# Moving roundings, weight splits, loads and transposes in a routed expert kernel

## What is computed

```python
x = x + cross(layernorm(x), ctx, mask)      # operands rounded to fp8, fp32 sum
h = layernorm(x)
idx, w = router(h)                           # 4 of 32 experts for each row
Xp = h[slots_token].reshape(E, C, d)         # E = 32 experts, C = 160 rows each
Y = (silu(Xp @ W_gate) * (Xp @ W_up)) @ W_down
out = zeros.at[slots_token].add(Y * slots_w)
shared = silu(h @ sg.T) * (h @ su.T) @ sd.T
x = x + out + shared
```

## Time and profile before

| | kernel before |
|---|---|
| executions, us | 1991.67, 1992.34, 1993.89 |
| the profiled execution, us | 1995.68 |
| its span, us | 1993.8 |
| TensorE clock granted, mean | 0.989 |
| PE busy, us (share of the span) | 1835.2 (92%) |
| DVE busy | 1390.6 (70%) |
| ACT busy | 865.1 (43%) |
| POOL busy | 601.7 (30%) |
| PE's share of the chain that ended last | 89% |

### The profile page before, as it was taken

The page is one execution under the profiler, slowest core; times in us unless marked ns, Lnnn a source line. Parts: engine busy times, 40 slices in busy tenths (PEclk is TensorE's granted clock), DMA queues, the critical chain, the costliest instruction groups (busy, mean ns, idle before and its releaser), DMA issues.

```text
span 1993.8 us, 44056 instructions
## 1 busy us (share of the span) xinstructions
PE 1835.2 (92%) x17380; PEld 1401.9 (70%) x17396; DVE 1390.6 (70%) x2509; ACT 865.1 (43%) x1209; POOL 601.7 (30%) x611
## 2 busy tenths in 40 slices
PE   0039999999999999999999999989999999999997
PEld 0017578668667767866866776778888888888886
DVE  5888685575566557557545644578888888888884
ACT  8564221222212212122221211357777777777773
POOL 2100211220220221122022022335655655656652
PEclk9989999999999999999999999999999999999999
DMA  9935534343433443434243245399999999999993
GB/s 377 395 96 171 148 72 109 100 102 86 106 97 75 106 118 69 112 97 103 67 106 75 54 106 143 82 344 365 353 368 360 353 370 358 354 370 349 366 367 82
DMA packets 188301, 395.45 MB, mean 198 GB/s; under 512 B 116304, under 2 KB 120432, under 8 KB 163600
## 3 DMA queue, kind: packets, MB, share of 16 engines
q1 hardware_dynamic: 163184, 334.77, 48.7%
q0 software_dynamic: 23808, 58.81, 13.5%
q10 hardware_dynamic: 1184, 0.15, 0.0%
HBM read 314.79 MB, written 55.35 MB: 186 GB/s over the span
## 4 chain that ended last, share of the span: by engine, by line
PE 89%; DVE 2%; issue 1%; DMA 1%; POOL 0%; ACT 0%; SPq 0%; DVEq 0%; POOLq 0%; ACTq 0%
PE ps L1334 54%; PE ps L1345 16%; PE ps L1517 8%; PE ps L1372 5%; PE ps L1525 2%; PE ps L1479 1%; PE ps L1420 1%; DVE W L1013 0%; DMA BIG<-in_w_gate 0%; PE ps L1484 0%; PE ps L1426 0%; DMA BIG<-in_sh_down 0%; POOL out_rows L606 0%; DVE BIG L941 0%; DVE BIG L940 0%
## 5 line engine op out<-in xcount | busy, mean ns | idle before, releaser
L1334 PE MATMUL ps<-XT,W 128*128 128x256 f16 (+1 forms) x12288 | 1114.2, 253 | 7.8 <-DVE SG L1302 3.8
L1334 PEld LDWEIGHTS ps<-XT,W 128*128 128x128 f16 x12288 | 1027.5, 98 | 92.0 <-issue 15.8
L1277 DVE SCALAR_TENSOR_TENSOR W<-BIG,W 128x2048 f16<-128x2048 f32 x192 | 435.9, 2284 | 64.7 <-ACT W L837 64.7
L837 ACT ACTIVATE W<-BIG 128x2048 f16<-128x2048 f32 x192 | 361.4, 1900 | 9.2 <-DMA BIG<-in_w_gate 8.8
L1345 PE MATMUL ps<-W,HH 128*128 128x512 f16 x1536 | 334.3, 379 | 1.8 <-DVE W L1013 1.8
L779 ACT ACTIVATE SG<-ps 128x256 f32<-128x256 f32 x128 | 49.0, 383 | 616.3 <-PE ps L1334 616.3
L1345 PEld LDWEIGHTS ps<-W,HH 128*128 128x128 f16 x1536 | 150.3, 98 | 182.9 <-issue 2.3
L257 POOL TENSOR_TENSOR expo<-expo 128x1 f32<-128x1 f32 x159 | 82.7, 520 | 633.0 <-ACT FR L708 266.5
L1192 DVE SCALAR_TENSOR_TENSOR SG<-ps,SG 128x256 f32<-128x256 f32 x128 | 54.2, 424 | 239.0 <-ACT SG L779 239.0
L539 POOL TENSOR_TENSOR rs<-ve,expo 128x1 f32<-128x1 f32 x32 | 17.6, 549 | 566.0 <-DVE ve L1034 566.0
L596 POOL DMA_INDIRECT FR<-xn_rows,gix x64 | 166.4, 2601 | 30.0 <-issue 30.0
(11 more groups left out here) (178 smaller groups left out, 1629.7 us busy)
## 6 DMA issues: line engine op xcount, KB each, us to landing
BIG<-in_w_gate SPq DMA_DIRECT2D x64, 1024.0 KB, 9.1
BIG<-in_w_up SPq DMA_DIRECT2D x64, 1024.0 KB, 8.2
BIG<-in_w_down SPq DMA_DIRECT2D x64, 1024.0 KB, 8.3
X<-in_x SPq DMA_DIRECT2D x16, 1024.0 KB, 5.0
X<-in_mask POOLq DMA_DIRECT2D x16, 1024.0 KB, 8.2
xn_rows<-FR SPq DMA_DIRECT2D x32, 512.0 KB, 3.6
out_rows<-X SPq DMA_DIRECT2D x32, 512.0 KB, 3.5
W<-in_x SPq DMA_DIRECT2D x6, 2048.0 KB, 19.6
```

Source lines behind the costliest of these rows:

```text
L837: ac.activation(dst, stage, ACT.Copy, scale=W_SCALE).then_inc(x_hi, 1)
L1277: ve.scalar_tensor_tensor(out=lo[cut], in0=src, scalar=W_SCALE, in1=hi[cut], op0=ALU.mult, op1=ALU.subtract).then_inc(x_lo, 1)
L1334: ins = te.matmul(out_ps, a[:, k, cols], b[:, k, :], start=n == 0, stop=n == len(steps) - 1)
```

## The change

In group 0, `x_round` moves from steps 4 and 5 to 3 and 4, the pieces 7 and 8 get steps of their own (2 and 3; 7 was at 1, and 8 was with 9 at step 5), 13 and 14 go from behind `residual` to step 7, and piece 12 is loaded ahead of SP's wait for the roundings. At the seam, expert 1's weights 0 to 3 are loaded ahead of the two stores of group 15 and 4 and 5 behind them, the gather of expert 0 goes ahead of four of POOL's index operations, the transposes of expert 0 go between matmul 15 and 16 of the last down product (u = 3), and `et_lo(0)` goes ahead of the last `add_shared`.

```diff
--- before.py
+++ after.py
@@ -280,7 +280,7 @@
         SW_PIECES = [(m, k, 4, ih) for ih in range(2) for m in range(2) for k in (0, 4)]
         SW_PIECES += [(2, k, 2, nh) for nh in range(2) for k in (0, 2, 4, 6)]
 
-        FIRST_SPLITS = [(4, 5), (6, 7), (), (), (), (8, 9), (10,), (11, 12), (13, 14, 15)]
+        FIRST_SPLITS = [(4, 5), (6,), (7,), (8,), (9,), (10,), (11, 12), (13, 14), (15,)]
         sw_dram = [sh_gate, sh_up, sh_down]
 
         LOADS = [("x", 0), ("b", 0), ("x", 1), ("x", 2), ("b", 1), ("x", 3), ("c", 0), ("x", 4), ("c", 1), ("x", 5),
@@ -385,6 +385,10 @@
             ctx_load(9, 1)
             ctx_load(8, 0)
 
+            def ew_load(e, m):
+                src = rows((w_gate, w_up, w_down)[m // 2], (e * 2 + m % 2) * P, P)
+                sp.dma_start(ew_stage[m], src).then_inc(ld_ew[m], 16)
+
             def xn_stores(f):
                 for j in range(NT):
                     wait(sp, a_xn, 2 * f + j + 1)
@@ -410,9 +414,10 @@
                     x_load(g + 1, 1 - r)
                 if first:
                     sw_load(11)
+                    sw_load(12)
                     sp.wait_ge(d_q, 4)
                     xq_transposes(1)
-                    for n in range(12, 16):
+                    for n in range(13, 16):
                         sw_load(n)
                     xn_stores_and_transposes(1)
                 if front and not first:
@@ -429,6 +434,11 @@
                 if front and not first:
                     xn_stores_and_transposes(g + 1)
                 for j in range(NT):
+                    if not front:
+
+                        for m in (2 * j, 2 * j + 1):
+                            sp.wait_ge(x_lo, m + 1)
+                            ew_load(1, m)
                     wait(sp, d_out, 4 * g + 2 * j + 2)
                     sp.dma_start(rows(out, g * G + j * P, P), xbuf[r][:, j, :]).then_inc(st_out[r], 16)
 
@@ -441,10 +451,6 @@
             for g in range(10, GROUPS - 1):
                 group(g, g % 2, ctx=max(12 - g, 0))
 
-            def ew_load(e, m):
-                src = rows((w_gate, w_up, w_down)[m // 2], (e * 2 + m % 2) * P, P)
-                sp.dma_start(ew_stage[m], src).then_inc(ld_ew[m], 16)
-
 
             sp.wait_ge(pe_xa, 4 * GROUPS)
             for m in range(6):
@@ -460,7 +466,10 @@
                 for c in range(TQ):
                     sp.dma_start(tab[c * TC:(c + 1) * TC, :, 1, :], slots[P:C]).then_inc(ld_tab, 16)
             group(GROUPS - 1, 1, front=False, ctx=0)
-            with sp.Fori(1, E) as e:
+            for m in (4, 5):
+                sp.wait_ge(x_lo, m + 1)
+                ew_load(1, m)
+            with sp.Fori(2, E) as e:
                 for m in range(6):
 
                     wait(sp, x_lo, e * 6 + (m - 5))
@@ -574,15 +583,9 @@
             ch.link(gp.tensor_scalar(tok[:, :], tab[:, :, 1, 0], float(T - 1), None, ALU.min))
             ch.do(gp.tensor_scalar(main(gidx[:, :]), tab[:, :, 0, 0], float(T - 1), None, ALU.min))
             ch.do(gp.tensor_scalar(tail(gidx[:, :]), tok[:, :], float(TQ), quarter[:, 0:1], ALU.mult, ALU.add))
-            ch.do(gp.tensor_copy(main(sidx[:, :]), tab[:, :, 0, 0]))
-            ch.do(gp.tensor_scalar(tail(sidx[:, :]), tab[:, :, 1, 0], float(TQ), quarter[:, 0:1], ALU.mult, ALU.add))
-            wts_cols = wts[:, :].rearrange("p (e u) -> p e u", u=3)
-            ch.do(gp.tensor_scalar(wts_cols[:, :, 0:2], tab[:, :, 0, 1].unsqueeze(2).to_broadcast([P, E, 2]), DOWN_PROJ, None,
-                                   ALU.mult))
-            ch.do(gp.tensor_scalar(wts_cols[:, :, 2], tab[:, :, 1, 1], DOWN_PROJ, None, ALU.mult))
             ch.sync()
             ch.close()
-            SLOT_STEPS = ch.before
+            GATHER_STEPS, SLOT_STEPS = ch.before, ch.before + 4
 
             def cols(e):
                 return bass.ds(e * 2, 2)
@@ -613,7 +616,15 @@
                 pool.wait_ge(st_xn[j], 16 * GROUPS)
             pool.wait_ge(d_lo, 2 * (GROUPS - 1))
             pool.wait_ge(t_xn, 64 * (GROUPS - 1))
-            gather(0, 0, SLOT_STEPS + 1, 2 * GROUPS)
+            gather(0, 0, GATHER_STEPS + 1, 2 * GROUPS)
+            ch.before += 1
+            ch.do(gp.tensor_copy(main(sidx[:, :]), tab[:, :, 0, 0]))
+            ch.do(gp.tensor_scalar(tail(sidx[:, :]), tab[:, :, 1, 0], float(TQ), quarter[:, 0:1], ALU.mult, ALU.add))
+            wts_cols = wts[:, :].rearrange("p (e u) -> p e u", u=3)
+            ch.do(gp.tensor_scalar(wts_cols[:, :, 0:2], tab[:, :, 0, 1].unsqueeze(2).to_broadcast([P, E, 2]), DOWN_PROJ, None,
+                                   ALU.mult))
+            ch.do(gp.tensor_scalar(wts_cols[:, :, 2], tab[:, :, 1, 1], DOWN_PROJ, None, ALU.mult))
+            ch.sync()
             gather(1, 1, SLOT_STEPS + 2, 2 * GROUPS + 1)
 
             for b in range(2):
@@ -1203,8 +1214,8 @@
                         route_picks()
                     if ic == (5 if front else 3):
                         route_weights()
-                    if front and ic - first in (3, 4):
-                        x_round(g + 1, ic - first - 3, M_main)
+                    if front and ic in (3, 4):
+                        x_round(g + 1, ic - 3, M_main)
                     if ctx and ic == 6 and not first:
 
                         ctx_round(g, 2 * g + 9, 1, 2 * g + 10)
@@ -1248,6 +1259,7 @@
                     ctx_round(0, 9, 1, 10)
                 if weights:
                     weights(3)
+                    et_lo(0)
                 add_shared(g, r, 3)
                 if first:
                     dve.wait_ge(d_cq, 10)
@@ -1287,7 +1299,6 @@
                 last = g == GROUPS - 1
                 group(g, g % 2, front=not last, ctx=max(12 - g, 0),
                       weights=(lambda n: ew_lo(0, 0, n)) if last else None)
-            et_lo(0)
             ew_lo(0, 0, 4)
             ew_lo(0, 0, 5)
 
@@ -1334,7 +1345,7 @@
                     ins = te.matmul(out_ps, a[:, k, cols], b[:, k, :], start=n == 0, stop=n == len(steps) - 1)
                 return ins
 
-            def down(out_ps, acts, weights, chunks, toks, cols, last_chunk=None):
+            def down(out_ps, acts, weights, chunks, toks, cols, last_chunk=None, between=None):
 
 
                 (hhi, hlo), (whi, wlo) = acts, weights
@@ -1342,6 +1353,8 @@
                 for n, (a, b, k) in enumerate(steps):
                     if last_chunk and n == 3 * (chunks - 1):
                         pe.wait_ge(*last_chunk)
+                    if between and n == 3 * (chunks // 2 + 1):
+                        between()
                     ins = te.matmul(out_ps, a[:, k, toks], b[:, k, cols], start=n == 0, stop=n == len(steps) - 1)
                 return ins
 
@@ -1399,6 +1412,24 @@
                         ins = te.transpose(PS[6 + h][:, k * P:(k + 1) * P], xn[j][:, (4 * h + k) * P:(4 * h + k + 1) * P],
                                            identf[:, :])
                     ins.then_inc(pe_xt, 1)
+
+            def et_transpose(e, b):
+
+                pe.wait_ge(ld_xg[b], (e - b) * 16 + 32)
+                for s in range(2):
+                    for k in range(4):
+                        ins = te.transpose(PS[2 + s][:, k * P:(k + 1) * P], xg[b][:, (4 * s + k) * P:(4 * s + k + 1) * P],
+                                           identf[:, :])
+                    ins.then_inc(x_xt, 1)
+                quarters = et_tail.rearrange("p (c q t) -> p q c t", c=TQ, q=2)
+                for q in range(2):
+                    ins = te.transpose(quarters[:, q], xgt[b][:, q * P:(q + 1) * P], identf[:, :])
+                ins.then_inc(x_xt, 1)
+
+            def first_rows():
+                pe.wait_ge(a_lg, GROUPS)
+                pe.wait_ge(d_route, GROUPS)
+                et_transpose(0, 0)
 
             def group(g, r, front=True):
                 if isinstance(g, int) and g == 0:
@@ -1450,7 +1481,8 @@
                         pe.wait_ge(sw_lo, 12 + 4 * u)
                     down(PS[4 + u % 2][:, :], hT, SW[2], KS, slice(j * P, (j + 1) * P),
                          slice(h * HALF, (h + 1) * HALF),
-                         last_chunk=(d_hl, 8 * g + 8) if u == 0 else None).then_inc(pe_dn, 1)
+                         last_chunk=(d_hl, 8 * g + 8) if u == 0 else None,
+                         between=first_rows if u == 3 and not front else None).then_inc(pe_dn, 1)
 
             pe.wait_ge(consts_ready, 2)
             for n, ready in ((0, x_root), (1, amax_ready)):
@@ -1470,24 +1502,6 @@
                 group(pair * 2 + 1, 1)
             for g in range(10, GROUPS):
                 group(g, g % 2, front=g < GROUPS - 1)
-
-            def et_transpose(e, b):
-
-                pe.wait_ge(ld_xg[b], (e - b) * 16 + 32)
-                for s in range(2):
-                    for k in range(4):
-                        ins = te.transpose(PS[2 + s][:, k * P:(k + 1) * P], xg[b][:, (4 * s + k) * P:(4 * s + k + 1) * P],
-                                           identf[:, :])
```

(10 more changed lines are left out.)

## The result

The changed kernel is faster, but by less than forecast. Thirteen timed executions beside thirteen of the kernel before gave medians of 1987.50 us and 1992.32 us, ratio 0.9979 with a 95% interval of 0.9972 to 0.9987. That is 4.8 us where 9.4 were forecast. The median lies above the span given with the forecast itself, 1981 to 1985, and inside the whole range of 1978.5 to 1988.0. Three later sets of executions of the same code gave 3.3, 3.3 and 2.9 us.

The account below looks back on a forecast made before the run. PE, busy 92% of the span, was taken as the bound, so only its standing or half clock could be won. Group 0's 2.2 plus the seam's 7.2 gave 9.4 us: median 1992.34 to 1982.9, range 1978.5 to 1988.0.

Parts of the forecast that it names:

- Group 0, the walk: Group 0: queues walked with measured durations; gain taken as 2.2 us, range -1 to 5.
- The stand at step 4: Group 0: PE newly stands 2.5 us near 175; costs nothing while DVE's queue is later, bound 0 to 1.
- the stand inside `cross`: Group 0: PE stands 4.3 us between the halves of cross, waiting for add_cross, and the clock falls.
- 8.6 us can be won: Seam: stretch from 1298.7 to 1329.5 takes 30.8 us against 22.2 undisturbed.
- the gain of 7.2: Seam: expert 1 starts at 1321.8 + 0.5 instead of 1329.5; range 1.5 to 7.7 us.
- The gather: Seam: gathered rows land at 1297.2, so PE stands 0.5 us ahead of expert 0's transposes, range 0 to 6.2.
- The mechanism I gave most room: Seam: DVE's ew_lo cast holds the first gather to 1291.9, so the second starts only 1.5 us earlier.
- The rule of the port: Seam: GpSimd cannot write descriptors while VectorE holds the shared port; first gather goes out about 1291.4, walk has 1291.9.
- The rule of the clock: PE: array falls to 1.2 GHz after an idle stretch; by it the 4.3 us stand must lose the clock.
- The clock holds: Rival, group 0: the clock holds or stands are split so it does; part gains 5, 1980.1 us; chance 0.12.
- The gather is late: Rival, seam: PE stands 3 us or more inside the down product; 1985.6 to 1991.6 us; chance 0.14.
- The second store: Rival, seam: store behind load 3 holds ACT and expert 0; 4 to 6 us slower, 1997; chance 0.04.

Follow-up runs that it names:

- the version that beats both: Changed kernel with pieces 7 and 14 moved back, loads 2 and 3 behind the second store, ACT's store wait moved to rows_out; 1978.28 against 1991.71 us.
- the loads held: Changed kernel with SP holding expert 1's loads 2 and 3 until expert 0's gathered rows have landed; 1990.24 against 1992.96 us.

## Why the prediction was wrong, point by point

**Group 0, the walk.** Right in its course. The stand at step 4 came (0.91, 3.69, 2.82, 2.86 us for 2.5 forecast), the transposes were no longer waited for, `add_cross` started at 206.02 (forecast 206.2), the stand inside `cross` was 4.75 us (4.3), group 1 started at 232.7 (233.9). The gain over four traces each is 2.3 us, forecast 2.2; over all traces with the old and the new group 0 (six and eight) it is 1.9, and the kernel with these edits alone gained 1.8 by its median (0 to 3.6). That it comes so near is in part luck: the walk's old cost (85.7) and its new one (83.7) both lie about 1 us above the means, 84.7 and 82.4, and that falls out of the difference. The walk said that the stand at step 4 costs nothing; in three of four traces it lost the clock for 3 to 7 us, and the second half of `cross` then started 0.4 to 1.2 us later than where the clock held. That is within the bound of 0 to 1 but for one.

**Group 0, what was not seen.** I took DVE's queue as given. Two entries of `FIRST_SPLITS` that the change had moved were costing some 4 us against what their old places allow (group 0: 78.4 and 78.6 us against a mean of 82.4; 75.3 in the version that beats both). The part's sum was right, and more than it forecast was left lying.

**The seam, the term that failed.** "8.6 us can be won", and from it the gain of 7.2. The walk of the seam after was nearly right: expert 1 started 46.4, 45.4, 45.2 and 45.4 us after group 15's down products began, where the walk has 44.4. What failed was the other side of the subtraction. The 51.6 us before rests on a stand of 3.84 us and the half clock behind it. In the other traces with that code the seam is 46.5 to 48.2: the first weights were there 5.7 to 7.5 us after their issue, where the prediction's trace had 9.1, and with stands of 0.4 to 2.2 us the clock was kept. This accounts for 3.9 us (51.6 against the 47.7 of the other three traces of the kernel), and the seam after, 45.6 us on average where the walk has 44.4, for another 1.2, most of it the late gather. What is left of the 7.2 is 2.1, and the kernel with the seam's edits alone gained 2.4.

There was a warning: the profiled execution took 1995.68 us, above each timed one, and it stayed above all thirteen of the comparison (highest 1993.89). I noted the 3.34 us and took the whole gain off the median all the same. A surplus of 3.3 us must sit somewhere in that trace, and stands that a DMA landing decides, with half clock behind them, are where it can sit. That the timed executions of that set had a cheaper seam is inferred, since they have no trace. Had the forecast carried the seam's old cost as a range of 46 to 52 us, its sum would have been about 4 to 10 us, and the measured 4.8 would have been in it, near the low end.

**The gather.** The term was 0.5 us (0 to 6.2); measured 2.31, 1.33, 0 and 1.33. The mechanism I gave most room, DVE's cast holding POOL, is the smaller part. In the changed kernel the gather's first indirect DMA began ahead of the cast and took 1.15 us, the second began in its midst and took 1.90 where a free one took 1.02, and both landed 8.1 and 8.7 us after issue, against 3.6 to 4.4 before. POOL's timeline, and the view of the gather's line in that stretch:

```profile
1286.01 1.15 POOL L599 DMA_INDIRECT FR<-xn_rows,gix  x1 [0.60 <-issue]
1287.46 1.90 POOL L599 DMA_INDIRECT FR<-xn_rows,gix  x1 [0.30 <-issue]
```

```profile
DMA to landing us min/median/max: 8.1/8.4/8.7
```

With loads 2 and 3 out of the way the stand was gone in each of five traces; with them in place it was there in six of eight. POOL was held in those five as in the changed kernel. The kernel with loads 2 and 3 behind the second store, where the second indirect DMA took 1.89 us, had this:

```profile
DMA to landing us min/median/max: 5.1/5.4/5.7
```

And the one with the loads held, with the longer hold by the cast:

```profile
1289.45 2.75 POOL L601 DMA_INDIRECT FR<-xn_rows,gix  x1 [0.30 <-issue]
```

```profile
DMA to landing us min/median/max: 6.7/6.8/6.9
```

So with the cast's hold alike, loads 2 and 3 made the landing 3 us longer (5.1 to 5.7 against 8.1 to 8.7), and the hold itself makes at most 1 to 3 us (3.6 to 4.4 without one, 5.1 to 6.9 with one, where loads 0 and 1 are under way too). It is the crowding on the DMA engines that makes the stand.

**The rule of the port.** The Trainium skill (SBUF — State Buffer, "SBUF: two separate sides") says the first comer of VectorE, with two SBUF inputs as this cast has, and a GpSimd operation that reads SBUF keeps the shared port for its whole instruction. GpSimd's side of it agrees: begun 0.17 us ahead of the cast, the first gather took 1.15 us, where one begun in the midst of a cast, at 1291.87, took 2.74. My walk had let the first one wait. VectorE's side does not show: the cast begun within that first gather took its usual 2.28 us.

**The rule of the clock.** The Trainium skill (TensorE: Matmul & The Clock Gate, "What's actually happening") has the array fall to half rate after an idle stretch. The traces agree that it falls, and length alone did not decide. Inside `cross`, a stand of 2.12 us lost the clock in the kernel with pieces 7 and 14 moved and the loads held, and one of 3.67 us kept it in the kernel with the loads held and ACT's wait moved; the granted clock, third from the end, of the two:

```profile
204.00:205.00 1.00, 1.00 (x4) 0.34 (x3) 0.96 (x4) 0.00 (x0) 0.43 (x1) 0.50 0.00 0
```

```profile
208.00:209.00 1.00, 1.00 (x6) 0.49 (x5) 1.00 (x2) 0.00 (x0) 0.00 (x0) 1.00 0.00 0
```

The stand forecast as 4.3 us came as 4.75, 2.37, 3.43 and 3.61 us in the four traces of the changed kernel, and lost the clock in all but the third. Elsewhere stands of 2.21 and 2.31 us kept it, and two of 1.61 and 1.78 us with 1.3 us of transposes between them lost it (the kernel with the early loads only). The prediction's argument, that 4.3 us is more than the 3.84 that lost it and 1.8 us kept it, was drawn from four stands of one trace. Neither side of it holds over all traces: the clock was lost after less and kept at 3.67 us. Only the stands of 3.84 us and more in these two stretches all lost it.

**The rivals.** "The clock holds" inside `cross` came in one of four traces of the changed kernel (the third, 81.2 us) and in two of all eight with its group 0. "The gather is late" came in mild form in three of four. "The second store" cost the two kernels with the loads held and ACT's wait in its old place some 4 us (seam 48.0 and 47.9 us, against 43.9 with the wait moved).

## What to carry to other kernels

A gain is a difference of two costs, and a single trace gives the old cost of one execution only: where the stands to be removed end with a DMA landing, or have half clock behind them, give them a range, above all if the profiled execution is slower than all timed ones. Transfers moved early share the engines with whatever is needed next: here two of four early loads delayed first a gather, then a store that ACT waited for. A wait for a store belongs at the first instruction that overwrites its source: here that gave back the 4.1 us that a late store cost where the loads were held (seam 48.0 and 43.9 us), and nothing showed where the loads stood behind the store (43.9 us either way). On the changed kernel by itself it was not tried.

## What the runs showed of the hardware

PE stands some 1.2 to 1.7 us in step 7 of group 15, in pieces, with nothing in the profile to release it; in these traces groups 1 to 15 take 1044.4 to 1046.2 us instead of 1042. It is in 12 of 18 traces, in both kernels, always within the last 30 matmuls or so of that step. And it goes with the set: it is in all twelve traces of the first, second and fourth set and in none of the four of the third, nor in the pair of the result. Kernels are compared within a set, so it should fall out of the medians, but traces of different sets differ by it. From the second trace of the kernel before:

```profile
1274.14 0.60 PE L1334 MATMUL ps<-XT,W 128*128 128x256 f16 x4 [0.18 <-issue]
1275.57 1.00 PE L1334 MATMUL ps<-XT,W 128*128 128x256 f16 x5 [0.83 <-issue]
1276.99 2.36 PE L1334 MATMUL ps<-XT,W 128*128 128x256 f16 x20 [0.42 <-issue]
```

What causes it was not tried and stays open, as does what makes one load of 1 MB land in 5.7 us in one execution and in 9.1 in another.
